# One block of latent attention and a routed FFN on one core: four lists of hand-ordered work are reordered, and the gathers at the end are spread differently

## The reference

```
x = x + layernorm(attention(layernorm(x)))
x = x + layernorm(ffn(layernorm(x)))
```

## Time and profile before

| | |
|---|---|
| median of 3 runs | 423.55 us (422.99 to 424.03) |
| the profiled execution: its own time | 423.33 us |
| its span, first to last instruction | 421.5 us |
| granted TensorE clock, mean | 0.995 |
| busy: TensorE / VectorE / ScalarE / GpSimd | 398.0 / 274.7 / 207.2 / 130.3 us |
| chain that ended last: TensorE / VectorE / GpSimd | 71% / 13% / 4% of the span |

### The profile page before, as it was taken

One profiled execution on the slowest core, in us unless ns is written; L12 is line 12 of the kernel. 1 busy time (PEld: TensorE's weight loads), 2 busy tenths in 40 slices (PEclk: granted clock), 3 DMA queues, 4 the chain that ended last, 5 costly groups with the idle time before them and its releaser, 6 DMA issues.

```text
span 421.5 us, 9545 instructions
## 1 busy us (share of the span) xinstructions
PE 398.0 (94%) x3443; PEld 301.2 (71%) x3443; DVE 274.7 (65%) x632; ACT 207.2 (49%) x381; POOL 130.3 (31%) x185
## 2 busy tenths in 40 slices
PE   8998999999999999898979999999999999998991
PEld 7775557676767776564859999999994443588991
DVE  5665777978878777866665693222226898725886
ACT  2645648585776667546451213344447676301110
POOL 2424515344251625303402002222212120036873
PEclk9999999999999999999999999999999999999998
DMA  7835236373635545450156741111111110123332
GB/s 257 225 107 146 65 89 185 92 223 95 213 92 154 159 109 191 103 182 26 30 176 218 248 135 34 30 44 45 52 50 51 47 44 27 53 68 112 117 94 100
DMA packets 50772, 47.29 MB, mean 112 GB/s; under 512 B 5350, under 2 KB 45542, under 8 KB 50726
## 3 DMA queue, kind: packets, MB, share of 16 engines
q1 hardware_dynamic: 44795, 38.31, 30.8%
q0 software_dynamic: 1632, 4.46, 3.7%
q10 hardware_dynamic: 4299, 3.92, 2.8%
HBM read 25.19 MB, written 8.65 MB: 80 GB/s over the span
## 4 chain that ended last, share of the span: by engine, by line
PE 71%; DVE 13%; issue 4%; POOL 4%; DMA 3%; ACT 3%; another core or an unknown queue 1%; SPq 0%; DVEq 0%; ACTq 0%; POOLq 0%
PE bank L1426 32%; PE bank L1758 7%; PE bank L1430 6%; PE bank L1603 5%; PE bank L1623 5%; PE bank L1564 4%; PE bank L1783 3%; DVE nmax L1098 2%; PE bank L1502 2%; PE bank L1550 2%; PE bank L1492 1%; DVE stacks L1396 1%; DMA x_sb<-x 1%; DVE wall L1128 1%; DVE stats_at L1002 1%
## 5 line engine op out<-in xcount | busy, mean ns | idle before, releaser
L1098 DVE TENSOR_REDUCE nmax<-bank 128x2 f32<-128x512 f32 x112 | 74.2, 685 | 27.4 <-PE bank L1564 26.7
L1426 PE MATMUL bank<-stacks,wall 128*128 128x128 f32 x512 | 61.5, 276 | 1.6 <-issue 1.2
L1426 PEld LDWEIGHTS bank<-stacks,wall 128*128 128x128 f32 x512 | 59.9, 192 | 3.9 <-issue 3.2
L1304 DVE TENSOR_TENSOR stacks<-stacks,bank 128x512 f32<-128x512 f32 x34 | 23.3, 685 | 53.2 <-PE bank L1426 47.3
L884 ACT ACTIVATE pv<-bank 128x512 f32<-128x512 f32 x64 | 38.3, 603 | 34.1 <-PE bank L1623 33.1
L920 ACT ACTIVATE stacks<-bank 128x512 f32<-128x512 f32 x34 | 20.3, 597 | 65.6 <-PE bank L1426 49.0
L884 ACT ACTIVATE wall<-bank 128x512 f32<-128x512 f32 x64 | 38.3, 606 | 24.9 <-PE bank L1623 24.8
L1426 PE MATMUL bank<-wall,stacks 128*128 128x256 f32 (+1 forms) x208 | 49.5, 381 | 1.1 <-DVE stacks L1304 1.1
L1623 PE MATMUL bank<-stacks 99*128 99x256 bf16 x256 | 48.8, 274 | 1.4 <-ACT wall L884 0.9
L716 POOL DMA_INDIRECT stacks<-x_sc,row_i x18 | 20.2, 1125 | 89.2 <-PE bank L1430 70.1
L1564 PE MATMUL bank<-stacks 96*128 96x256 bf16 x224 | 42.3, 273 | 4.8 <-DVE nmax L1098 4.7
(11 more groups left out here) (213 smaller groups left out, 801.9 us busy)
## 6 DMA issues: line engine op xcount, KB each, us to landing
stacks<-low_sb SPq DMA_DIRECT2D x144, 64.0 KB, 2.0
wall<-gate_up SPq DMA_DIRECT2D x8, 1024.0 KB, 5.3
wall<-down SPq DMA_DIRECT2D x8, 512.0 KB, 6.6
y_exp<-stacks ACTq DMA_DIRECT2D x18, 128.0 KB, 1.7
x_tok<-wall SPq DMA_DIRECT2D x8, 256.0 KB, 2.5
stacks<-x_tok SPq DMA_DIRECT2D x16, 128.0 KB
out<-stacks SPq DMA_DIRECT2D x8, 256.0 KB
stacks<-low_sb SPq DMA_DIRECT2D x12, 128.0 KB, 2.4
```

The lines of the kernel that those rows point to most:

```text
L1098: dve.tensor_reduce(nmax[:, half, qt, 2 * pair:2 * pair + 2], two(sm_bank[u % 2]), AX.X, ALU.max, negate=True).then_inc(sm["sm_max"], 1)
L1304: dve.tensor_tensor(to, sg, fu[:, :], ALU.mult).then_inc(sm["h_sb"], 1)
L1426: last = pe.matmul(out_ap, lhsT, rhs, start=(n == 0), stop=(n == len(pairs) - 1))
```

## The change

Four things change, all in order only. No instruction is added or removed.

1. GpSimd: two pairs of gathers instead of three are issued before the finals. The pair for step 2 follows the power of step 0; the pairs for steps 3 and 4 both follow the power of step 1; the rest stays (5 after power 2, 6 after 3, 7 after 4).
2. VectorE: the scaled tiles `c:10` and `c:11` come ahead of the router's logits of slot 7 and the one-hots.
3. TensorE, at the start of its list: `E_xn2T:6` comes ahead of `PV3:7`, and `U:1` ahead of `D_wo:7`.
4. TensorE, near its end: `I:0` stood between `U:6` and `Y:5` and now stands behind `G:7`. (The change's own short name says "place products sooner"; in the list the word I:0 moves back by two words.)

```diff
-                for c in range(3):
+                for c in range(2):
                     gather(c)
...
-            after_power = {c: c + 3 for c in range(HALF - 3)}
+            after_power = {0: (2,), 1: (3, 4), **{c: (c + 3,) for c in range(2, HALF - 3)}}
...
                 power("out", c + 1, rstd_f[:, p, :], var_f[:, p, :], 2)
-                if c in after_power:
-                    gather(after_power[c])
+                for n in after_power.get(c, ()):
+                    gather(n)
...
             play(steps, "D_div0:7 c:4 c:5 E_router:6 D_div1:7 h:0 c:6 c:7 c:8 c:9 D_y:7 h:1 D_yn:7 D_stats:7 h:2 E_xn2:7"
-                        " E_router:7 O:1 c:10 c:11 h:3 g:1 c:12 c:13 c:14 c:15 p:1 n:0 h:4 m:0 h:5 l:0 l:1 l:2 l:3 e:0 h:6 r:0 q:0"
+                        " c:10 c:11 E_router:7 O:1 h:3 g:1 c:12 c:13 c:14 c:15 p:1 n:0 h:4 m:0 h:5 l:0 l:1 l:2 l:3 e:0 h:6 r:0 q:0"
...
-            play(steps, "PV3:7 E_xn2T:6 D_avT0:7 E_router:6 D_avT1:7 G:1 D_aT:7 D_wo:7 U:1 Y:0 G:2 U:2 Y:1"
+            play(steps, "E_xn2T:6 PV3:7 D_avT0:7 E_router:6 D_avT1:7 G:1 D_aT:7 U:1 D_wo:7 Y:0 G:2 U:2 Y:1"
                         " E_xn2T:7 G:3 E_router:7 U:3 K:1 Y:2 G:4 U:4 Y:3 G:5 U:5 Y:4"
-                        " G:6 U:6 I:0 Y:5 G:7 U:7 Y:6 X:8 Y:7 GR:8 X:9")
+                        " G:6 U:6 Y:5 G:7 I:0 U:7 Y:6 X:8 Y:7 GR:8 X:9")
```

## The result

The changed kernel took 424.88 us, the median of 19 runs (423.73 to 427.45), beside 423.61 for the kernel before (19 runs, 422.18 to 424.83). The ratio is 1.0034, interval 1.0022 to 1.0046: slower by 1.4 us (the medians differ by 1.3). The forecast of 427.7 had the sign and missed the size by 2.8; the time lies where the rival of the vanished late signal put it (424.4). The profiled execution took 424.47 with a span of 422.6 and a granted clock of 0.996.

A forecast was written before the change was run, and what follows sets the result against it. TensorE was taken to bound the first stretch, GpSimd's add of x, its store and VectorE's waiting adds the end. 1.93 + 2.45 = +4.4 on the profiled 423.33 gave 427.7 us, range 424.2 to 429.2.

The forecast's parts named there:

- the rival of the vanished late signal: Final step 1: VectorE's 3.50 wait for TensorE goes away, the end gains 0.9, time 424.4; chance 0.17.
- Parts 1 to 4: TensorE from last scores to first routed tile: list edits cost 1.10 - 0.67 + 1.25 + 0.25 = +1.93, carried to the end.
- Part 3: VectorE's c:10 and c:11 ahead of E_router:7: fall into its wait for the router's product, cost 0.
- Part 5: Gathers at the end: two pairs behind power(1) delay plus_x(1) by 2.50 and every later step; cost +2.45.
- The second rival: Final step 1: TensorE's late signal goes away with fewer gathers in a row, end gains 0.9, time 424.4; chance 0.17.
- The rival of the short add: Step 4's long VectorE add does not come again: the end costs +1.2 instead of +2.45, time 426.5; chance 0.2.
- Faster: End: signal on time, steps follow TensorE and not GpSimd's queue; all of 3.5 gained, time 421.8; chance 0.08.
- the prediction's last rival: Four gathers in a row at step 1 call up a second late signal, up to 3.5; with 2, 429.7; chance 0.1.

The follow-up runs named there:

- the lists alone: Kernel before with the three list edits (turn, up product, place products, scaled tiles), gathers as before: 425.94 us, ratio 1.0051.
- the single edits: Kernel before with one edit each: E_xn2T:6 ahead of PV3:7 (+1.05 us), U:1 ahead of D_wo:7 (+0.2), I:0 behind Y:5 and G:7 (+0.8).
- turn: Kernel before with only E_xn2T:6 moved ahead of PV3:7: 424.93 us, ratio 1.0025.
- up: Kernel before with only U:1 moved ahead of D_wo:7: 424.25 us, ratio 1.0005.
- the better version with the old order: Kernel before with x added on VectorE and a reordered TensorE list, three pairs of gathers still ahead: 420.46 us without the late signal, 424.20 with it.
- the gather part: Kernel before with only the change's new order of gathers: 422.58 us (ratio 0.9971) with the late signal, 422.48 (1.0023) without.
- the pause: Kernel before with GpSimd waiting until two gather pairs landed before issuing the third: 423.10 us (1.0053) without the late signal, 422.57 (0.9951) with it.
- group 3: Kernel before, gathers' edit alone, whole change and a better version, run on another chip without the late signal; kernel before 421.45 us.

## Why the prediction was off

**Parts 1 to 4 held** as a sum, and in where the waits stand. Beyond the 0.46 that the trace of after brought along, TensorE began X:8 2.0 later (263.15 against 260.66); the sum said 1.93, the lists alone measured +2.1, and the single edits +1.05, +0.2 and +0.8. The waits came where they were put and with the right releasers: 1.12 for 1.10 before PV3:7, 1.26 for 1.25 before E_xn2T:7, 0.43 for 0.25 before X:8. Part 3's nought was not measured alone.

**Part 5 failed, in two of its sentences.** It said +2.45; the trace of after shows -1.4, and the part measured alone is -1.2 with the late signal and +1.0 without. That the sign of the whole came out right is the lists' doing, whose loss of 2.1 outweighs this gain.

The first is that freeing power(0) is "worth nothing", since VectorE "sits 3.50 waiting for a signal of TensorE's there". The wait was taken as a fixed feature of the kernel. It is an effect of what the part edits. On the chips where the kernel before takes 424, all five profiled kernels with three pairs ahead and no pause have it, 3.5 to 4.3 long (before, lists, turn, up, and the better version with the old order); the three others (the change, the gather part, the pause) have none at that step. The pause shows it most narrowly, since it keeps the three pairs and changes only their timing. The second rival had this mechanism and priced it well: it gave 0.9 of gain at the add plus_x(1), and from the first gather to that add the trace of after is 394.50 - 377.45 = 17.05 against 392.89 - 374.94 = 17.95 before. (By its own terms, 392.89 - 391.9, it should have said 1.0, and 424.3.) It got a chance of 0.17 because "nothing in the kernel's order explains it"; a wait that nothing explains, in the very place that is edited, deserved more.

The second is "No slack stands in between". It can be judged without the signal, in group 3. There power(0) comes sooner for the pair that is no longer ahead of it, and VectorE, which had waited 0.96 for it, uses that; so plus_x(1), at 392.99 against 390.59, is 1.62 late beyond the 0.78 of this trace, and not 2.50. At VectorE's last products 1.27 is left. So the block of two pairs does delay the end, and about half of its 2.50 is given back.

**The rival of the short add is out.** The second add of the late step took 2.17 in the changed kernel, 2.19 and 2.18 in the gather part alone. The prediction set this row against the rule of the Trainium skill's page "SBUF — State Buffer" (section "SBUF: two separate sides"), by which whichever of the two engines starts first keeps the shared ports for its whole instruction. The recorded starts again have VectorE first: its add is recorded from 398.44, GpSimd's from 399.05, and VectorE's ends at 400.61, behind GpSimd's end at 400.32. But these rows do not refute the rule, as the prediction took them to. At its usual 0.42 VectorE's add would have ended at 398.86, before GpSimd's recorded start, so whatever held it was at work earlier than that start says. GpSimd had a gather on at that moment (398.06 to 399.02), but a gather alone does not do it: beside one, with no add behind it, the same add took 0.42 (395.32, in the version with x added on VectorE). Which engine had the ports first stays open.

**Faster** did not come about: the chain still runs through GpSimd's add and its store. **A second late signal** behind the four gathers in a row did come, and the prediction's last rival had named it, but it is 1.2 long and not up to 3.5, and it falls where VectorE has to wait for power(2) anyway, so the rival's price of 2 was nought.

**The size of the change depends on the chip.** The changed kernel takes 424.9 and 425.1 in its two groups, and the gather part alone 422.6 and 422.5. The kernel before takes 423.6 to 424.3 in three groups and 421.1 to 421.5 in the three others (counting the first comparison as a group). The forecast was drawn from one trace with the late signal. Where it is absent, the change costs 4.1 (3.1 to 5.1), an interval that holds the 4.4 forecast and, at its lower end, the sum of the parts measured alone (2.1 and 1.0); so it does not bear out the 2.45 of part 5.

**A version that beats both.** Two pairs ahead, x added on VectorE and the reordered list take 420.8 twice. It is 0.1% faster than the kernel before where that has no late signal (ratios 0.9985 and 0.9993, the second with an interval that holds 1). It was not run on a chip with the signal; that it would keep its time there, as the gather part did (422.6 and 422.5), is argued and not shown.

**What stays open**: why TensorE's signal is late, and why only on some chips. The runs show what calls it up and what removes it, not the path on which it is held. Theory P puts it down to the third pair being issued while the first two are in flight, but the pause also moves that pair behind the end of the up product (382.05 against 377.66 + 3.73 = 381.39). In the traces with a late signal the product ends while a row of gathers is being issued (six at step 1, four at step 3), and where four in a row had been issued 1.4 before the product ended (gathers to 382.16, product to 383.57, kernel after) it was on time. Whether it is the number in flight or the moment was not tested apart.

## What to carry to other kernels

A wait that no instruction explains is not part of the terrain: before it is used as cover for an edit beside it, ask what else is in flight at that moment, and give its vanishing a chance of its own. A word may move ahead of another in a hand-written list only if its inputs are ready at the new place; the timeline gave the price of the three such moves here within 0.6 us, about what these runs can tell. When 0.3% matters, measure the kernel before on the same chip, and on more than one chip, since the same program differed by 0.7% between them through one wait.

## What the runs showed of the hardware

- On some chips TensorE's completion reached VectorE and SyncE 3.8 us after the product's recorded end (VectorE 4.6 in one kernel) when the product ended in a row of six gathers of 128 rows issued 1.25 us apart. In a row of four it reached VectorE 1.2 to 1.3 us after the end, in two traces. It came within 0.4 (VectorE was busy until then) when the last of four had been issued 1.4 us before the end and the next came after it. On the other chips even eight in a row left it on time.
- VectorE's add of two SBUF inputs took 1.07 to 2.23 us and not 0.42 in 18 rows where GpSimd's 128x512 add of x (1.26 to 1.29) ran beside it, whichever of the two was recorded first, and it ended 0.3 behind that one each time. Beside a gather alone it kept its 0.42. With x added on VectorE, two 128x256 adds did in 0.76 what GpSimd did in 1.28, and none of VectorE's adds of routed results was stretched.
